# Three places in the order of a recommendation tower's chunks: the last added tile, the relu of z2, the row numbers

## The reference

```python
for i, (W, b) in enumerate(zip(Ws, bs)):          # W0: 128 outputs, W1: 128, W2: 1
    z = jnp.einsum('bhd,bmd,ohm->bod', h, x, W.reshape(O, H, F))
    z = jax.nn.relu(z + b[None, :, None])
    if i < n_layers - 1:
        h, direct = (z[:, :half, :], z[:, half:, :])   # 64 go on, 64 are summed
    else:
        direct = z
    directs.append(direct)
z = jnp.sum(jnp.concatenate(directs, axis=1), axis=-1)
h = jnp.concatenate([z, dense_ctx], axis=1)
h = jnp.maximum(h @ W_top1 + b_top1, 0.0)
h = jnp.maximum(h @ W_top2 + b_top2, 0.0)
y = h @ W_top3
```

## Time and profile before

| | |
|---|---|
| median of 3 runs | 1190.58 us (1186.73 to 1193.34) |
| profiled execution, its own time | 1200.2 us |
| its span, first to last instruction | 1198.4 us |
| TensorE / VectorE / ScalarE / GpSimd busy | 1117.0 / 1018.3 / 646.4 / 614.3 us |
| mean granted TensorE clock | 0.982 of full speed |
| DMA | 226.27 MB, 189 GB/s over the span |

### The profile page before, as it was taken

How to read it: one execution, slowest core, us unless ns; L and a number is a source line. 1 busy time by engine, 2 the same in 40 slices (tenths; PEclk the granted TensorE clock), 3 DMA queues, 4 the chain that set the end, 5 groups by cost and what they waited for, 6 DMA issues and landing times.

```text
span 1198.4 us, 12182 instructions
## 1 busy us (share of the span) xinstructions
PE 1117.0 (93%) x3736; PEld 682.1 (57%) x3736; DVE 1018.3 (85%) x636; ACT 646.4 (54%) x607; POOL 614.3 (51%) x398
## 2 busy tenths in 40 slices
PE   0789999999899998899898998999999998999998
PEld 0356666656556665556565665656566565656654
DVE  2789999999798988799797997999999898989953
ACT  0445566555456654366563656565654665556544
POOL 5645565555466564466743657455545666421100
PEclk9989999999899999999998999999999999999999
DMA  6787877787787767788667887778887776777730
GB/s 196 206 233 198 224 203 190 188 206 206 185 219 174 210 179 192 174 220 217 170 169 185 207 221 176 190 180 226 216 213 193 199 205 181 189 210 183 162 58 0
DMA packets 86455, 226.27 MB, mean 189 GB/s; under 512 B 15313, under 2 KB 36050, under 8 KB 86434
## 3 DMA queue, kind: packets, MB, share of 16 engines
q1 hardware_dynamic: 57602, 152.23, 40.7%
q0 software_dynamic: 26624, 71.33, 32.4%
q10 hardware_dynamic: 2208, 2.45, 0.7%
HBM read 99.98 MB, written 8.39 MB: 90 GB/s over the span
## 4 chain that ended last, share of the span: by engine, by line
PE 41%; DMA 23%; POOL 12%; issue 10%; ACT 7%; DVE 4%; SPq 2%; POOLq 0%; DVEq 0%; ACTq 0%
PE z_ps L646 40%; DMA add_lo<-raw_add 18%; POOL gathered L305 11%; DMA x_roll<-x_dram 4%; ACT h_roll L846 2%; ACT prod_hi L878 2%; ACT add_lo L886 2%; SPq L394 1%; POOL add_lo L313 1%; DVE prod L473 1%; ACT add_hi L885 1%; ACT direct L850 1%; DVE raw_add L534 1%; DVE raw L519 1%; PE mlp_ps L646 1%
## 5 line engine op out<-in xcount | busy, mean ns | idle before, releaser
L646 PE MATMUL z_ps<-prod,w_sb 128*128 128x512 f32 x1280 | 580.9, 601 | 32.1 <-DVE prod L605 27.4
L305 POOL DMA_INDIRECT gathered<-in_table,rows_sb x256 | 482.8, 1886 | 131.6 <-issue 64.5
L646 PEld LDWEIGHTS z_ps<-prod,w_sb 128*128 128x128 f32 x1280 | 247.9, 194 | 295.9 <-issue 283.5
L313 POOL DMA_DIRECT2D add_lo<-raw_add x128 | 123.8, 967 | 386.0 <-ACT add_lo L886 384.7
L885 ACT CAST add_hi<-raw_add 128x1024 fp32r<-128x1024 f32 x128 | 133.8, 1045 | 274.4 <-DVE raw_add L534 145.2
L526 DVE TENSOR_TENSOR prod_lo<-raw,prod_hi 128x2048 fp32r<-128x2048 f32 x96 | 219.7, 2289 | 58.2 <-ACT prod_hi L878 56.2
L519 DVE TENSOR_TENSOR raw<-h_roll,x_roll 128x2048 f32<-128x2048 f32 x96 | 219.8, 2289 | 1.8 <-DMA h_roll<-h_roll 0.6
L473 DVE TENSOR_TENSOR prod<-h_roll,x_roll 128x2048 f32<-128x2048 f32 x96 | 219.1, 2282 | 0.0
L878 ACT CAST prod_hi<-raw 128x2048 fp32r<-128x2048 f32 x96 | 182.1, 1897 | 8.6 <-DVE raw L519 7.8
L534 DVE TENSOR_TENSOR raw_add<-h_roll,x_roll 128x1024 f32<-128x1024 f32 x128 | 155.8, 1218 | 30.4 <-DMA add_lo<-raw_add 30.4
L473 DVE TENSOR_TENSOR prod<-x_base,x_roll 128x2048 f32<-128x2048 f32 x63 | 144.2, 2289 | 22.7 <-DMA x_roll<-x_dram 14.8
(11 more groups left out here) (66 smaller groups left out, 624.2 us busy)
## 6 DMA issues: line engine op xcount, KB each, us to landing
x_roll<-x_dram SPq DMA_DIRECT2D x128, 512.0 KB, 8.3
add_lo<-raw_add POOLq DMA_DIRECT2D x128, 512.0 KB
x_base<-x_dram SPq DMA_DIRECT2D x32, 512.0 KB
h_roll<-h_roll SPq DMA_DIRECT2D x32, 448.0 KB
h_roll<-h_roll SPq DMA_DIRECT2D x32, 384.0 KB
h_roll<-h_roll SPq DMA_DIRECT2D x32, 320.0 KB
x_dram<-gathered SPq DMA_DIRECT2D x64, 128.0 KB, 3.5
x_part<-x_dram SPq DMA_DIRECT2D x64, 128.0 KB, 8.1
```

The lines of the kernel that those rows point to most:

```text
L305: nc.gpsimd.indirect_dma_start(gathered[:, u % 2, g * DIM:(g + 1) * DIM], None, table, bass.IndirectOffsetOnAxis(ap=rows_sb[:, col:col + 1 ...
L313: nc.gpsimd.dma_start(add_lo[:, k % ADD_RING, :], raw_add[:, k % ADD_RING, :], accum_op=ALU.add).then_inc(add_lo_ready[k % ADD_RING], 16)
L646: return nc.tensor.matmul(*args, **kw)
```

## The change

No instruction is added or taken out, but for one wait. The order changes at these places:

- VectorE: `add_product(3)` moves behind `split_product(2)` and `products1(2)`, so to just before `split_rest(2)` (in steps u = 1 before `sum_z2`).
- ScalarE: `round_added(3)` moves behind `round_products(2)`. `relu2` moves from the end of the step u = 0 to the next step, u = 1, between `relu1` and `round_added(1)`; TensorE's last `layer2_sum` is served by a `relu2` in the tail, as before.
- SyncE: roll 2 is loaded before roll 3, whose release now comes later.
- ScalarE's `relu0(c)` also waits for all added products of chunk c - 2, whose last read of h now comes behind the products for which `relu0` waited before.
- GpSimd: in steps u = 1, `make_rows` stands behind `add_raw(0)`, not before it.

```diff
@@ GpSimd, step
+                add_raw(0, ready[0])
+                if ahead:
                     if u == 1:
                         make_rows(group + 1)
-                add_raw(0, ready[0])
-                if ahead:
                     gather((u + 3) % UNROLL, made, freed, range(0, 3))
@@ SyncE, step
                 if two_ahead:
+                    load_roll(c + 2, s, 2)
                     load_roll(c + 2, s, 3)
-                    load_roll(c + 2, s, 2)
@@ VectorE, step
                 split_rest(c, u, 1)
-                add_product(c, u, 3)
                 split_product(c, u, 2)
                 products1(c, u, 2)
+                add_product(c, u, 3)
                 if u == 1 and not_first(c, UNROLL):
                     sum_z2(group - 1)
                 split_rest(c, u, 2)
@@ ScalarE, relu0
                 if not_first(c, 2):
                     act.wait_ge(prod_ready, first1(c - 2) + WHOLE1)
+                    act.wait_ge(raw_add_ready, (c - 1) * ADDED1)
@@ ScalarE, step
                     relu1(c - 1, (u - 1) % UNROLL)
+                    if u == 1 and not_first(c, UNROLL):
+                        relu2(group, group - 1)
                     round_added(c, 1)
...
                 round_products(c, u, 1)
                 round_added(c, 2)
+                round_products(c, u, 2)
                 round_added(c, 3)
-                round_products(c, u, 2)
-                if u == 0 and not_first(c):
-                    relu2(group, group - 1)
```

## The result

| | before | after |
|---|---|---|
| median of 19 runs each | 1190.95 us (1176.79 to 1210.82) | 1179.0 us (1163.22 to 1188.98) |
| profiled execution, its own time | 1200.2 us | 1173.95 us |
| mean granted TensorE clock, profiled | 0.982 | 0.987 |

The ratio is 0.9887, 95% interval 0.9847 to 0.9927: 1.1% faster. The forecast was 1163, 2.3% under the median of before; the direction came, and half of the size.

The account below looks back on a forecast made before the run. TensorE was taken as the bound, sometimes held up by the DMA and GpSimd path. From 1200.2 us, minus 35.6 for slow steps and 6.5 for tile 2 gives 1158, plus 5 gives 1163; range 1152 to 1196 (8 in 10).

Parts of the forecast that it names:

- The slow steps: Seven of 29 steps, 5.1 us too long each through a late second transfer; their removal was to save 35.6 us.
- the term of 6.5: TensorE's wait for tile 2: its transfer lands sooner without roll 3's load beside it, 6.5 us taken of 13.
- forecast T + 15.8: Tile 3's transfer in chunk 23, T = 870.80 at relu0's start: issued at 886.6 against 884.79, no lateness taken.
- The rival of a late tile 3: Tile 3's transfer takes over 8.0 us and TensorE waits every step: 1193 at 9.2 us, 1207 at 9.7; chance 0.10.
- I add one slow step, 5 us: Allowance in the sum for a thin margin in the 14 steps u = 3 and u = 0: 1158 becomes 1163.
- So VectorE waits at least 0.2 us there: At the second products0, VectorE arrives at 891.7, before TensorE frees its slot at 891.9, so the gather runs quickly.
- Roll 3, which was to widen the margin: Roll 3, issued at about 884.0, lands at 892.3 by the 8.3 us median; VectorE needs it at the second products0.
- It does not do what it says: Rival: as many slow steps as before, only 6.5 us gained at tile 2, giving 1184; chance 0.12.
- loses its turn: Rival: VectorE no longer waits at the second products0; all 14 steps u = 3 and 0 slow, 1229; chance 0.10.
- The condition: In steps u = 3 and 0, slow when VectorE runs without wait from add_product(0) to product16: gather idle 2.01 to 2.03.
- nothing on the path: relu2's move in steps u = 1: first transfer earlier, any VectorE gain hidden behind TensorE, so no time counted.
- the rival "held": make_rows is held as chunk 27's gather was; second transfer late in seven steps u = 1, 1194; chance 0.10.

Follow-up runs that it names:

- the two kernels with pauses: Kernels before and after, each with three VectorE waits on its own last result, before products1(0), split_rest16 and split_rest(0): 1169.78 us (before), 1160.77 us (after).
- tile and relu: Kernel after with make_rows back in front of add_raw(0), keeping the moves of the last added tile and relu2: 1172.33 us, ratio 0.9883.
- the relu alone: Kernel before with only relu2's move to step u = 1: 1201.92 us, ratio 1.0104, not resolved.
- late pauses: Kernel after with three VectorE waits on its own last result, placed behind split_product(1), too late for the first gather: 1160.72 us, ratio 0.9775.
- that edit and the pauses: Kernel before with three VectorE waits on its own last result, and SyncE loading roll 2 before roll 3, nothing else: 1173.29 us, ratio 0.9869.
- the tile part alone: Kernel before with only the last added tile's VectorE, ScalarE and SyncE moves and relu0's wait: 1169.31 us, ratio 0.9804.
- with pauses the relu is worth 6.4 us: Kernel before with three VectorE self-waits and the last added tile's move, 1166.32 us; kernel after with these waits and make_rows back before add_raw(0), 1159.92 us.
- the row numbers alone: Kernel before with only make_rows moved behind add_raw(0) in steps u = 1: 1227.98 us, ratio 1.0296.

## Why the prediction was half right

**Right.** The slow steps are the main cost of the kernel before, and their mechanism is the one named: the held gather, a second transfer 14.4 us behind the first, and TensorE's wait. That VectorE's timing decides it was right too. Tile 2's wait halved: 0.24 us a step less, 7.8 us in the profile and 9.0 us between the two kernels with pauses, against the term of 6.5. No wait for prod_hi stands before `split_rest(2)` (858.10, against 0.53 us in the earlier trace rows). Tile 3's transfer goes out at T + 15.9 us (forecast T + 15.8) and no matmul on it waits: in the step shown it is used 7.5 us after its issue. The rival of a late tile 3 is wrong.

**The step that failed** is "I add one slow step, 5 us", and behind it "So VectorE waits at least 0.2 us there". In the step shown VectorE comes to the second `products0` at T + 20.95 (865.84), where I had 891.7, T + 20.9. TensorE was to free the slot at T + 21.1. But its first matmul on tile 2 starts at T + 15.8 (860.68), against T + 17.0 less the wait of 1.00 in the earlier trace rows: 0.2 us earlier than assumed, all that the margin was. Roll 3, which was to widen the margin, didn't: the median of the rolls from issue to landing fell from 8.3 to 6.5 us, and in this step VectorE shows no wait for it. In this trace five of the steps u = 3 and u = 0 have a gather with 2.00 to 2.03 of idle time, one of them held; in u = 2 there is one such gather, and it is held. "The margin is thin" should have been a price: with 18 us measured in place of 5, this term takes 13 of the 16 us between 1163 and 1179.0. Nearest to what was measured is the rival "It does not do what it says", 1184, by the mechanism of the rival "loses its turn": not more often than before, but nearly as often. And the sum counted slow steps in the 14 steps u = 3 and u = 0 alone, where the profile has one of its three.

**The other 3 us** are in the start of the sum. 1200.2 - 35.6 = 1164.6 should be the kernel before without slow steps, and 1169.8 was measured with pauses, 5 us more; the larger gain of the order (9.0 for 6.5) gives half of it back.

**The condition** was half found. An idle time of 2.0 is needed for the hold, but half of such gathers run quickly. That "in steps u = 2 [...] an idle time of 2.02 goes with 1.25 us" is no property of u = 2: chunk 18 after, chunks 6 and 10 in tile and relu, chunks 22 and 26 in the relu alone, and four steps with late pauses were held at u = 2. What the four of before had was VectorE's wait at the first `products0`. The prediction took what VectorE does after `add_product(0)` for the whole condition, and the stretch ahead of it has a part as well.

**The cause of tile 2's gain** was wrong: roll 3's load has no part in it (0.55 us a step with that edit and the pauses). Nor was relu2's move "nothing on the path". It takes away what TensorE waited in steps u = 1 (0.72 to 0.33 us), and seems to let slow steps back: the tile part alone has a ratio of 0.9804 and two held gathers, tile and relu 0.9883 and four, though with pauses the relu is worth 6.4 us (1166.32 to 1159.92, two sets of runs, with intervals of the ratios that overlap). The intervals of the first pair overlap, so this stays likely, not shown.

**`make_rows`** behind the transfer was the rival "held", and came true in part: one instruction of 7.45 us, one slow step of 39.49. The rule cited from the Trainium skill (SBUF — State Buffer, Who interferes with whom) agrees on who is held. The trace shows GpSimd kept out past several VectorE instructions (869.30 to 875.29, four starts), where the section speaks of one instruction. The rule alone would have every such gather wait, and 34 of the 68 took 1.25 us beside the same instructions, so it is not the whole condition.

## What to carry to other kernels

When runs of one kernel spread by 3%, look in the trace for a step that comes in two lengths, and count it in several executions before pricing it: a sum made from one profile takes its number of slow steps for the kernel's. A hold that depends on whether an engine happens to wait is not cured by an order that makes it wait by 0.2 us. A semaphore wait of the engine on itself took 0.2 us of its slack here, and no gather was held behind it. Look also at what the delayed transfer runs into, because here the delay was harmless when the transfer went out before the next large load. And when a condition read from a few steps seems to spare one kind of step, look for what those steps had in common further back.

## What the hardware did that I had not expected

- GpSimd's gather (usually 1.25 us) took 5.98 to 6.00 us when held, and its `tensor_tensor` of 128 x 32 integers (0.3 to 2.7 us elsewhere) took 7.45 us once, beside back-to-back VectorE `tensor_tensor`. In the two steps shown the end comes 0.1 us (`make_rows`) and 0.9 us (gather) after a gap of only 0.04 us between two VectorE instructions.
- With the same idle time, 34 of 68 first gathers were held: 2 of the 27 with a wait of VectorE 9.0 us ahead, 32 of the 41 whose last wait lay further back. Why a wait so far ahead matters, and what decides in the 11 exceptions, stays open.
- A wait of VectorE on its own last instruction costs 0.2 us from start to start (1.14 to 1.35), and none of 52 first gathers beside one was held, where 34 of 68 were without it.
- The clock falls with TensorE's wait, but not by its length alone. The three slow windows after were granted 0.91 to 0.96. Right behind waits of 3.81 and 4.10 us two matmuls of 512 columns took 1.22 us, at the lower level, 1.2 GHz (0.62 in a quick step); behind one of 3.64 us they took 0.73. In the kernel before 1.22 us stands behind a wait of 3.08 us, and in the row numbers alone 0.75 behind 3.90.
